# Gated feed-forward: rows of pairs 2 to 4 transposed on VectorE, silu as one ScalarE function, down products around p4 and p3

## The reference

```python
x = x + tanh(g_xattn) * attention(layernorm(x), ctx, ctx)      # 16 heads of 32, 4 weights of 512 x 512
x = x + tanh(g_ffn) * ffn(layernorm(x))

def ffn(x):                      # w_gate, w_up: 1536 x 512, w_down: 512 x 1536, integers times 1/127
    gate = x @ w_gate.T
    up = x @ w_up.T
    return (silu(gate) * up) @ w_down.T
```

## Time and profile before

| | |
|---|---|
| runs | 874.02 us (873.65 to 874.04, 3 runs) |
| profiled execution | 874.07 us, span of its instructions 872.3 us |
| TensorE's granted clock | 1.00 of full speed (2.4 GHz) throughout |
| busy: TensorE, VectorE, ScalarE, GpSimd | 98%, 75%, 53%, 46% |
| feed-forward part | 372.5 us to the end |
| of that: seven products | 1344 matmuls |
| of that: down products | 768 matmuls |
| of that: transposes of x2 | 128, of them 32 for the first pair |

### The profile page before, as it was taken

One profiled execution on the slowest core, in us unless ns is written; L12 is line 12 of the kernel. 1 busy time (PEld: TensorE's weight loads), 2 busy tenths in 40 slices (PEclk: granted clock), 3 DMA queues, 4 the chain that ended last, 5 costly groups with the idle time before them and its releaser, 6 DMA issues.

```text
span 872.3 us, 12869 instructions
## 1 busy us (share of the span) xinstructions
PE 855.0 (98%) x4087; PEld 707.9 (81%) x4087; DVE 652.8 (75%) x1081; ACT 460.5 (53%) x1130; POOL 402.3 (46%) x344
## 2 busy tenths in 40 slices
PE   8999999999999999999999999999999999999997
PEld 7678888888888887788888888888888888888876
DVE  5988877778786877679688478788487877587882
ACT  5687575666666757446056264165362364460550
POOL 4665555556564664437144444155253255251350
PEclk9999999999999999999999999999999999999999
DMA  9233847272728131567333256043265143243302
GB/s 334 73 109 118 276 152 248 84 240 93 233 97 277 68 113 51 198 235 265 115 123 133 96 190 249 12 165 121 79 248 182 47 164 113 96 166 116 97 31 98
DMA packets 60406, 128.73 MB, mean 148 GB/s; under 512 B 7616, under 2 KB 20416, under 8 KB 60352
## 3 DMA queue, kind: packets, MB, share of 16 engines
q1 hardware_dynamic: 58960, 125.95, 41.7%
q10 hardware_dynamic: 1392, 2.10, 0.7%
HBM read 99.93 MB, written 27.79 MB: 146 GB/s over the span
## 4 chain that ended last, share of the span: by engine, by line
PE 87%; DVE 6%; ACT 3%; issue 1%; DMA 1%; POOL 1%; ACTq 0%; DVEq 0%
PE psum L1814 34%; PE psum L1548 29%; PE psum L1864 18%; PE psum L1573 4%; DMA gates<-g_ffn 1%; PE psum L1657 1%; ACT e L791 1%; POOL hT L696 1%; DVE bn L1034 1%; DVE e L1076 1%; DVE K L1128 1%; DVE mx L1073 1%; DVE qT L1058 0%; DVE pT L1047 0%; DVE aT L1058 0%
## 5 line engine op out<-in xcount | busy, mean ns | idle before, releaser
L1814 PE MATMUL psum<-xv,ring 128*128 128x512 f32 x1344 | 308.2, 390 | 0.9 <-ACT a L964 0.7
L1814 PEld LDWEIGHTS psum<-xv,ring 128*128 128x128 f32 x1344 | 251.5, 188 | 55.1 <-ACT a L964 1.1
L696 POOL TENSOR_TENSOR hT<-th,hT 128x512 fp32r<-128x512 f32 x48 | 86.3, 1798 | 201.2 <-ACT hT L984 201.2
L1864 PE MATMUL psum<-w_d,hT 128*128 128x512 f32 x768 | 177.7, 391 | 1.3 <-POOL hT L696 0.8
L1864 PEld LDWEIGHTS psum<-w_d,hT 128*128 128x128 f32 x768 | 143.7, 188 | 32.6 <-POOL hT L696 2.0
L554 POOL TENSOR_TENSOR e<-e,rden 128x616 f32<-128x616 f32 x64 | 77.9, 1217 | 110.4 <-DVE rden L1110 73.8
L791 ACT ACTIVATE e<-psum,nmx,q_scale 128x77 f32<-128x77 f32 x256 | 102.6, 427 | 2.3 <-DVE nmx L1090 2.2
L952 ACT ACTIVATE a<-psum 128x512 f32<-128x512 f32 x48 | 28.7, 599 | 131.7 <-PE psum L1814 131.4
L1428 DVE SCALAR_TENSOR_TENSOR acc<-psum,gate_ffn,acc 128x512 f32<-128x512 f32 x64 | 47.7, 750 | 65.1 <-PE psum L1864 65.1
L1548 PE MATMUL psum<-wo,aT 128*128 128x512 f32 x384 | 95.2, 399 | 0.5 <-DVE aT L1058 0.5
L1548 PE MATMUL psum<-xT,wq 128*128 128x512 f32 x360 | 89.0, 398 | 0.4 <-DVE qT L1058 0.4
(11 more groups left out here) (110 smaller groups left out, 1204.6 us busy)
## 6 DMA issues: line engine op xcount, KB each, us to landing
ring<-w_var SPq DMA_DIRECT2D x48, 896.0 KB, 4.6
w_var<-stage SPq DMA_DIRECT2D x12, 896.0 KB, 4.6
x_ln<-x SPq DMA_DIRECT2D x32, 256.0 KB, 4.6
x_res<-x SPq DMA_DIRECT2D x32, 256.0 KB, 5.0
x_mid<-x_res SPq DMA_DIRECT2D x32, 256.0 KB, 2.0
x<-x_mid SPq DMA_DIRECT2D x16, 512.0 KB, 5.6
acc<-x_mid SPq DMA_DIRECT2D x16, 512.0 KB, 6.4
out<-acc SPq DMA_DIRECT2D x32, 256.0 KB, 2.0
```

The lines of the kernel that those rows point to most:

```text
L696: nc.gpsimd.tensor_tensor(hT[:, 1, i % HH, j, :], h[:, :], hT[:, 0, i % HH, j, :].bitcast(f32), ALU.subtract).then_inc(h_lo, 1)
L1814: last = nc.tensor.matmul(psum[:, bank, :], stat, mov, start=start and j == 0, stop=j == len(terms) - 1, skip_group_check=not start)
L1864: last = nc.tensor.matmul(m_bank[t % 2][:, :], hT[:, a, m, t // TT, (t % TT) * P:(t % TT + 1) * P], w_d[:, HH * h + m, :], start=m == 0 an ...
```

## The change

Four things are changed, all in the feed-forward part.

1. For pairs 2 to 4 (p + 1 = 1 to 3) TensorE's `turn` is gone. VectorE transposes instead, `turn_rows`: 16 instructions for each block of 512 rows, each taking a quarter of the partitions (32) and the same quarter of all columns, 512 elements in each of its 32 partitions, in blocks of 32 x 32, from x2 into `x2_t`, which lies in SBUF. `xv_round` (ScalarE), `form` and `xv_low` (VectorE) read x2_t instead of PSUM for these pairs. The first 16 instructions of a pair stand in `first_half`, two behind each result; the other 16 in iterations 7 to 10, four behind `hidden2` in each. The statistics move from `first_half` to iterations 3 to 6, two tiles each; `normalise2` of the first block goes ahead of the results.
2. silu is ScalarE's function Silu; VectorE's `silu1` and `silu2` are gone. The factor in `gate_ffn` changes accordingly.
3. At the end of a pair TensorE does: four slots of tile 0, p4(last), four slots of tile 1, p3(last), four slots of tile 2, slot 4 of tiles 0 to 2, slot 5 of tiles 0 to 2, then tiles 3 to 7. Tile 2 of the second half has a bank of its own, `set_c[0]`.
4. ScalarE's roundings of the next pair's rows stand behind the last `h_high`, and VectorE's `xv_low` of B11 and T1 behind the last `hidden2`.

The memory layout follows: x2_t takes the room of b12 and a new place behind the ring, and the mask `causal` lies in a shared region. The core of the diff:

```diff
@@ gpsimd, pair @@
-                    if p + 1 < NP and m == HH - 1:
-                        rstd_ahead(2 * p + 2)
-                        rstd_ahead(2 * p + 3)
+                    if p + 1 < NP and m in (HH - 2, HH - 1):
+                        rstd_ahead(2 * p + m - HH + 4)
@@ scalar @@
+            def xv_round(q, j):
+
+                full, half_of, free = {B11: (b11, 0, p1_full), B21: (b21, 0, p2_full), B22: (b22, 1, p3_full)}[j]
+                act.wait_ge(x2_turned, turned(half_of, q))
+                act.wait_ge(free, MH * q)
+                if j == B22:
+                    act.wait_ge(v_formed, nth(FORMED, q, T3))
+                nc.scalar.activation(xv[:, j, 0], full, ACT.Copy).then_inc(xv_hi, 1)
...
-                nc.scalar.activation(th1[:, :], psum[:, set_a[i % 2], :], ACT.Tanh, scale=0.5 * W_SCALE)\
-                    .then_inc(tanh1_done, 1)
+                nc.scalar.activation(th1[:, :], psum[:, set_a[i % 2], :], ACT.Silu, scale=W_SCALE)\
+                    .then_inc(silu1_done, 1)
...
-                if more:
-                    xv_copy(p + 1, B11, b11_at)
-                tanh2(last)
-                tanh1(last)
-                if more:
-                    b12_copy(p + 1)
+                silu2(last)
+                silu1(last)
                 h_high(last, 0)
                 h_high(last, 1)
                 if more:
+                    xv_round(p + 1, B11)
                     xv_high(p + 1, T1)
-                    xv_copy(p + 1, B21, b21_at)
+                    xv_round(p + 1, B21)
                     xv_high(p + 1, T2)
                     xv_high(p + 1, T3)
                     xv_high(p + 1, T4)
-                    b22_copy(p + 1)
+                    xv_round(p + 1, B22)
@@ vector @@
+            def turn_rows(q, half_of, ops):
+
+                tiles = slice(TT * half_of, TT * half_of + TT)
+                dve.wait_ge(x2_normed, PT * (q - 1) + TT * (half_of + 1))
+                if q > 1:
+                    dve.wait_ge(v_formed, nth(FORMED, q - 1, T4))
+                for op in ops:
+                    a, c = divmod(op, HG)
+                    rows = x2[a * HD:(a + 1) * HD, tiles, :].rearrange("p t (k n) -> p t k n", n=P)
+                    to = x2_t[half_of][c * HD:(c + 1) * HD].rearrange("p k (t n) -> p t k n", n=P)
+                    nc.vector.transpose(to[:, :, :, a * HD:(a + 1) * HD], rows[:, :, :, c * HD:(c + 1) * HD])\
+                        .then_inc(x2_turned, 1)
...
+                    one, other = b12, b11 if q else pair_of(b11_at)
...
+                nc.vector.tensor_tensor(lo, one, other, ALU.subtract).then_inc(v_formed, 1)
...
+                full = {B11: b11, B21: b21, B22: b22}[j] if q else pair_of(bank)
+                nc.vector.tensor_tensor(xv[:, j, 1], full, xv[:, j, 0].bitcast(f32), ALU.subtract)\
                     .then_inc(xb_lo, 1)
...
             def first_half(p, more):
+                if more:
+                    normalise2(2 * p + 2)
                 for t in range(PT):
-                    if more:
-                        stats2(2 * p + 2 + t // TT, t % TT)
...
                     result(p, 0, t)
-                    if more and t >= PT - 2:
-                        normalise2(2 * p + 2, range(2 * (t - PT + 2), 2 * (t - PT + 2) + 2))
-                if more:
-                    normalise2(2 * p + 3)
+                    if more:
+                        turn_rows(p + 1, 0, (2 * t, 2 * t + 1))
+                    if more and t in (5, 6):
+                        normalise2(2 * p + 3, range(2 * (t - 5), 2 * (t - 5) + 2))
...
                     if m:
-                        silu2(i - 1)
-                        silu1(i - 1)
                         hidden1(i - 1)
                         upper2(i - 1)
                         hidden2(i - 1)
...
+                    if more and 3 <= m <= HH:
+                        for t in (2 * m - 6, 2 * m - 5):
+                            stats2(2 * p + 2 + t // TT, t % TT)
+                    if more and HH < m < MH - 1:
+                        turn_rows(p + 1, 1, range(4 * (m - HH - 1), 4 * (m - HH)))
                 gate2(last)
-                silu2(last)
-                if more:
-                    xv_low(p + 1, B11, b11_at)
-                silu1(last)
                 hidden1(last)
                 upper2(last)
                 hidden2(last)
-                if not more:
-                    widest()
-                if more:
-                    form(p + 1, T1)
+                if more:
+                    xv_low(p + 1, B11, b11_at)
+                    form(p + 1, T1)
+                else:
+                    widest()
                 result(p, 1, 0)
                 result(p, 1, 1)
@@ tensor, pair @@
-                if more:
-                    turn(p + 1, B11)
-                    turn(p + 1, B12)
+                early, late = range(HH - 2), range(HH - 2, HH - 1)
+                down(p, 1, 0, early)
                 p4(last)
+                down(p, 1, 1, early)
                 p3(last)
-                down(p, 1, 0, range(HH - 1))
-                down(p, 1, 1, range(HH - 1))
+                down(p, 1, 2, early)
+                for t in range(3):
+                    down(p, 1, t, late)
...
-                down(p, 1, 0, range(HH - 1, HH))
-                down(p, 1, 1, range(HH - 1, HH))
-                if more:
-                    turn(p + 1, B22)
-                    turn(p + 1, B21)
-                for t in range(2, PT):
+                for t in range(3):
+                    down(p, 1, t, range(HH - 1, HH))
+                for t in range(3, PT):
                     down(p, 1, t)
```

More of the change, by code:

```diff
@@ L338, in pair_of, with turned, down_bank @@
             return psum[:, bank:bank + 2, :]
+        TURNS = HG * HG
+        def turned(half, q):
+            return TURNS * (2 * (q - 1) + half + 1)
+        def down_bank(h, t):
+            return psum[:, set_c[0], :] if (h, t) == (1, 2) else m_bank[t % 2][:, :]
         block = ctx.enter_context(nc.Block())
@@ L939, in _ @@
                     xv_high(0, T1)
-            xv_copy(0, B21, b21_at)
+            xv_copy(B21, b21_at)
             xv_high(0, T2)
@@ L993, in pair @@
                     if m:
-                        tanh2(i - 1)
-                        tanh1(i - 1)
+                        silu2(i - 1)
+                        silu1(i - 1)
                     snap2(i)
@@ L1247, in form @@
             def form(q, j):
                 lo = xy[:, j, 1]
+                if q:
+                    dve.wait_ge(x2_turned, turned(1, q))
+                    dve.wait_ge({T1: p5_full, T2: p6_full, T3: p7_full, T4: p4_full}[j], MH * q)
+                else:
+                    if j == T1:
+                        dve.wait_ge(b12_kept, 1)
+                    dve.wait_ge(xb_full, nth(TURNED, 0, {T1: B11, T2: B22, T3: B22, T4: B21}[j]))
+                if j == T2:
+                    dve.wait_ge(v_formed, nth(FORMED, q, T1))
@@ L1257, in form @@
-                    ins = nc.vector.tensor_tensor(lo, pair_of(b22_at), xy[:, T1, 1], ALU.subtract)
+                    one, other = b22 if q else pair_of(b22_at), xy[:, T1, 1]
                 if j == T3:
-                    ins = nc.vector.tensor_tensor(lo, pair_of(b22_at), b12[:, :, :], ALU.subtract)
+                    one, other = b22 if q else pair_of(b22_at), b12
                 if j == T4:
-                    dve.wait_ge(xb_full, nth(TURNED, q, B21))
-                    dve.wait_ge(v_formed, nth(FORMED, q, T2))
@@ L1263, in form @@
[L1263 to L1264 removed]
+                    one, other = b21 if q else pair_of(b21_at), xy[:, T2, 1]
+                nc.vector.tensor_tensor(lo, one, other, ALU.subtract).then_inc(v_formed, 1)
             def xv_low(q, j, bank):
                 dve.wait_ge(xv_hi, nth(HI_ORDER, q, j))
[L1269 removed]
+                full = {B11: b11, B21: b21, B22: b22}[j] if q else pair_of(bank)
@@ L1451, in first_half @@
             def first_half(p, more):
+                if more:
+                    normalise2(2 * p + 2)
                 for t in range(PT):
-                    if more:
-                        stats2(2 * p + 2 + t // TT, t % TT)
-                    elif t < HH:
+                    if not more and t < HH:
                         dve.wait_ge(rd_used, HH)
@@ L1781, in step @@
                     o(3)
-                    turn(0, B11)
-                    turn(0, B12)
+                    turn(B11)
+                    turn(B12)
                 q(1)
@@ L1801, in _ @@
                 if m == 1:
-                    turn(0, B22)
-            turn(0, B21)
+                    turn(B22)
+            turn(B21)
             pe.wait_ge(m_free, M_LAST + 4)
@@ L1857, in down @@
                 if slots[0] == 0:
-                    m_wait(i)
+                    if (h, t) == (1, 2):
+                        pe.wait_ge(c12_done, MH * p + MH - 1)
+                    else:
+                        m_wait(i)
```

(4 more changed lines are left out.)

117 lines of the change are left out of this document (45 added, 72 removed).

## The result

The changed kernel takes 899.26 us (median of 4 runs, 898.65 to 900.39), the kernel before beside it 873.88 (4 runs, 873.65 to 874.04): a ratio of 1.0295, interval 1.0282 to 1.0308. The forecast was 888.3 us with a range of 871 to 901: the sign, the waits and the two engines at one port came as forecast, but the loss was 11.2 us short, and two of its causes, TensorE's clock and the pitch of its products, were not in the sum. The profiled execution has a span of 897.7 us against 872.3, which is 25.4 us more.

The account below looks back on a forecast made before the run. TensorE, 98% busy, was taken as the bound. Each of three pairs: -3.5 - 0.27 + 1.1 + 7.6 = +4.95 us; with -0.65 in the last, +14.2 on 874.1 gave 888.3 us, range 871 to 901.

Parts of the forecast that it names:

- What leaves TensorE: 32 transposes go at three pair ends, 3.5 us each; with covered waits in all pairs, a gain of 12.3 us.
- The first wait of a pair end: Tile 3 wants tile 1's bank at 9.98 us, but VectorE finishes result(1,1) at 12.6: TensorE waits 2.63 us.
- The port: At pair ends VectorE's subtracts and GpSimd's low parts exclude each other at SBUF; tile 5 waits 3.98 us, tile 6 0.80.
- Rival 1: VectorE keeps the SBUF port at pair ends until a real gap: 5.4 us per pair end, 881.7 us; chance 0.14.
- rival 2: The SBUF port matters little: waits of 3.5 us per pair end, 876 us (872.7 with overlapping transposes); chance 0.14.
- The loop of iterations 7 to 10: VectorE and ScalarE loop with four transposes takes 6.62 us against TensorE's 6.35: 1.1 us for each of three pairs.
- Rival 3: A VectorE transpose costs more than 0.70 us: 898 us in all at 0.9 us, 929 at 1.22; chance 0.15.
- The statistics of the first pair: Moved to iterations 3 to 6, 2 x 0.87 us each, they just fit into 6.35 us beside the weights' maxima.
- ScalarE and the loads: Silu costs the same as before, a second table load 0 (at most 1.3 us); x2 loads land 0.7 us early.
- the signs: Expected if right: period 129 us, acc waits 20 us or more, subtracts over 2.5 us, iterations 7 to 10 at 6.6.
- The likeliest case of the prediction: Pair-end waits of 7.6 us, with contested port, and the transpose loop outweigh the transposes removed: 884 to 892 us, 0.42.
- The faster case: VectorE's queue stays ahead of TensorE everywhere, needing 2.6 us less and a free port: 862 us; 0.15 including anything up to 872.

Follow-up runs that it names:

- experiment 9: Changed kernel with only the conversions of the next pair's rows (roundings, low parts, T1 to T4) taken forward at the pair end: 882.98 us, ratio 1.0106.
- experiment 1: Changed kernel with GpSimd's low parts of T1 to T4 (pairs 2 to 4) held until VectorE has formed T4: 886.71 us, ratio 1.0151.
- experiment 5: Changed kernel with the ring 128 bytes up, 104,192 bytes behind xv: 897.18 us, ratio 1.0265.
- Experiment 10: Changed kernel with ring 128 bytes up, GpSimd held, transposes split, conversions earlier, plus tile 3 in another bank, T3 later, statistics split: 865.38 us, ratio 0.9905.
- experiment 7: Kernel before with only Silu in place of Tanh and VectorE's two combining instructions removed: 871.82 us, ratio 0.998.
- 8: Changed kernel with ring 128 bytes up, GpSimd's low parts behind T4, one transpose of four ahead of hidden1, and earlier conversions: 868.08 us, ratio 0.9941.
- 4: Changed kernel with everything moved up by 208 bytes, ring and xv at unchanged distance: 899.5 us, ratio 1.0299.
- 6: Changed kernel with one of the four transposes of iterations 7 to 10 moved ahead of hidden1: 894.23 us, ratio 1.0245.

## Why the prediction was right, and where it fell short

**What leaves TensorE: right.** No transpose of pairs 2 to 4 is left on it. In the last pair the waits of 0.69 and 0.26 us of the earlier trace rows are gone, and the one of 0.50 has become 0.69 (forecast 0.8).

**The first wait of a pair end: right.** Forecast 2.63 us, measured 2.61, from the layout of VectorE's queue behind p3. Its reason was right too, that the transposes and the early rounding of before had covered the conversions: experiment 9 takes the conversions forward, and the wait is 1.30.

**The port: right in every length, one wait too large.** Forecast: xv_low of B21 2.76 us, T4 3.35, result(1,3) done 22.2 us behind p7. Measured: 2.76, 3.39 and 22.4. Rival 1 falls with it: GpSimd's waiting instruction gets the port ahead of VectorE's next one, though that is ready. So does rival 2: experiment 1 measures 4.2 us a pair for the port, where the prediction had 4.1 between its own case and this rival. What failed is the other side of the sum: TensorE reached tile 5 later than 18.27 us, since it ran part of tiles 3 and 4 at the lower clock, so it waited 2.52 us there instead of 3.98, and the 0.80 at tile 6 was absorbed. Where the clock stayed up, in experiment 5, that wait was 3.63.

The Trainium skill (SBUF — State Buffer, SBUF: two separate sides) has VectorE and GpSimd share a port pair under an exclusive lock for a whole instruction. The trace agrees: 2.76 and 3.39 us for instructions that take 1.21 and 1.22 when GpSimd is held back.

**The clock: not in the sum at all.** At the end of the first pair the 24 matmuls behind the first wait took 7.07 - 5.61 = 1.5 us more than at full clock, and the 36 behind the second 10.07 - 8.34 = 1.7 us more. I had priced each wait at its own length. Forecast waits 7.6 us a pair end; measured 5.1 us of waits, 3.2 us of slower matmuls and 0.3 us in which the last matmul ahead of each wait runs out (0.39 us for a pitch of 0.227), 8.7 in all. The term was 1.0 us short. That it came so close is luck: the slower matmuls stood in for waits that they shortened. The other two pair ends have 26.8 us for the 80 down products as well.

**The loop of iterations 7 to 10: right in kind, 0.3 us a turn short.** The 6.62 us had four transposes at 2.80; from the first one's start to the next addition it is 2.94, at a pitch of 0.725 us for a duration of 0.703. Most of the rest stands on both sides of hidden2: 0.79 us from upper2's start to hidden2's for 0.69, and 0.72 from there to the first transpose for 0.61, since neither overlaps. Four turns, with the slow pitch in what lies in front of them and behind, make 2.77 us instead of 1.1, so 1.7 us a pair. Rival 3 falls: the transpose was sized rightly.

By the Trainium skill (VectorE: DVE Perf Modes, Two Vector instructions with no wait between them) transposes whose outputs start in other groups of 32 partitions should not overlap, and the pitch of 0.725 us agrees.

**The pitch of the products: missing.** I took 0.227 us from the earlier trace rows as a constant of the instruction and did not look at where the change puts its operands, though the change moves buffers in front of the ring. It is 0.97 us in the first part of each of three pairs and 1.9 us in the last pair, 4.8 us together.

**The statistics of the first pair: "just fit" did not.** Pair 1 took 0.95 us more than pair 2; its 188 products have a chain that leaves TensorE in iterations 3 to 5, where the maxima of the weights and the statistics share VectorE. Experiment 10, which splits them, has 42.82 us for that stretch.

Together: 3 x (1.7 + 0.97 + 0.8) = 10.4, the first pair 1.0, and the last pair 1.3 (0.6 measured for -0.65) make 12.7 us above the forecast (whose own terms add up to 4.93 us a pair, not 4.95); outside the pairs some 1.3 us were gained, which leaves 11.4 for the 11.2 us that it fell short. Of those 1.3 us 1.2 lie behind the last down product; why that end got shorter was not tried. The 0.8 is the 1.0 of the waits less 0.3, since the wait for hT that went was worth 0.55 us and not 0.27 (experiment 7). In the last pair, too, the new order saved more than I had put, 1.3 us for 0.65, which hides a part of the pitch's 1.9; in part this is because the idle times of the earlier trace rows leave out how far a matmul outlasts its pitch.

**ScalarE and the loads: right.** Experiment 7 has the second table load at no cost. It did hold back the first silu, whose input was ready at 378.66 us while it starts at 380.12, but not TensorE. The statistics of iteration 3 in the first pair start at 397.74 us behind busy VectorE, with no wait for the loads.

The Trainium skill (ScalarE: Activation LUTs, What ACT_TABLE_LOAD costs) puts the load itself at about 1283 ns, and a switch with its drain at about 2.66 us. The trace agrees with the first, 1.283 us, and shows nothing of the second: the silu starts 1.29 us behind the start of the load.

**The chances and the signs.** The likeliest case of the prediction, 884 to 892 us at 0.42, did not come. 899.26 us lies where it had put rival 3, over 892 us at 0.15, and rival 3 is false: a transpose takes 0.703 us. So the place of the time within the range owes nothing to the mechanism given for it. Of the signs, subtracts over 2.5 us came; TensorE's waits for acc, at 20 us or more, did not, they are 15.6 us with the last pair's; the period is 132.4 us and not 129, and the loop 6.93 and not 6.6.

**The faster case.** Its 862 us was missed by 3.4 us by the kernel of experiment 10. The kernels of 8 and 10 meet most of its condition, VectorE 2.6 us ahead and the port free, by other means.

## What to carry to other kernels

When work moves from TensorE to another engine, lay out the queue that it leaves: the transposes covered conversions that nobody had to wait for, and without them the same conversions stood ahead of the results that free the banks. Price a wait of TensorE at its length and at the slower matmuls that may follow, and keep waits short rather than few in total (experiment 9: 2.2 us of waits in two pieces, none of the 3.2 us of slower matmuls). And when a change moves a buffer, compare the matmul pitch of stretches without a wait before anything else, for every pair of operands: here it was 7.9 us of the kernel before for 2,432 bytes, and the cure of one pair of operands slowed another.

## What the runs showed of the hardware that I had not expected

- A 128x512 Strassen product of this kernel takes 227.3 to 227.7 ns when its stationary operand lies a multiple of 256 bytes from the moving one (101,632 and 104,192), and 232.7 ns at 128 more than a multiple (104,064); common shifts of both by 208 and 1,232 bytes did nothing. With the products of pT and V it was the moving operand alone that moved, from 66,560 to 66,688 bytes, and 288 products took 1.4 us longer. Two remainders only were tried.
- TensorE's granted clock fell from 1.00 to 0.50 for 3 to 4 us behind all six waits at the pair ends of the changed kernel (2.2 to 2.6 us long), though it had been at 1.00 ahead of them. In experiments 1, 4, 5 and 6 it fell behind 14 of 21 waits of 2.2 to 3.6 us, once for 7 us, and waits of 2.6 us are on both sides. No wait of 1.4 us or less at a pair end (experiments 8 to 10) brought it. What decides is open.
- On the port that VectorE and GpSimd share, an instruction of GpSimd that waits is served before VectorE's next one, also where VectorE has no gap: 1.2 us of work takes 2.76 and 3.39 us.
